# Moving the next step's scores, and two of the four down quarters, within TensorE's order of work

## The reference

```
h = layernorm(x) * (1 + ca) + sa
x = x + ga * attention(h)         # 16 heads of 8, causal, window of 32 keys
h = layernorm(x) * (1 + cb) + sb
x = x + gb * moe(h)               # 8 experts of 128 -> 256 -> 128
# moe: gate scores, the best 2 of 8 weighted by a softmax; per expert
#      y_e = layernorm(h + gelu(h @ w1_e + b1_e) @ w2_e + b2_e) * g_e + b_e
#      out = sum over e of weight_e * y_e
```

## Time and profile before

| what | value |
|---|---|
| median of 3 runs (lowest to highest) | 275.79 us (274.9 to 275.96) |
| the profiled execution's own time | 275.96 us |
| its span | 274.2 us |
| granted TensorE clock, mean | 0.966 of full speed |
| PE busy | 239.3 us, 87% |
| weight loads (PEld) busy | 206.0 us, 75% |
| DVE, ACT, POOL busy | 184.4, 159.8, 134.6 us |

### The profile page before, as it was taken

The page is one execution under the profiler, slowest core; times in us unless marked ns, Lnnn a source line. Parts: engine busy times, 40 slices in busy tenths (PEclk is TensorE's granted clock), DMA queues, the critical chain, the costliest instruction groups (busy, mean ns, idle before and its releaser), DMA issues.

```text
span 274.2 us, 7792 instructions
## 1 busy us (share of the span) xinstructions
PE 239.3 (87%) x3064; PEld 206.0 (75%) x3064; DVE 184.4 (67%) x570; ACT 159.8 (58%) x419; POOL 134.6 (49%) x254
## 2 busy tenths in 40 slices
PE   7985884999999989998999989999999899989970
PEld 4653554988888878887888878888888788767960
DVE  2778469548596758666876769485967585456075
ACT  2354402784579375956487548844893769455650
POOL 8065436024670477146732675256714770468075
PEclk9979896899999999999999999999999999999996
DMA  6930000000000000000000000000000000000000
GB/s 203 332 151 0 2 4 1 0 4 2 4 19 2 4 2 0 19 6 0 4 19 2 2 2 20 4 4 2 19 2 2 2 1 19 6 0 0 22 0 20
DMA packets 5652, 6.23 MB, mean 23 GB/s; under 512 B 336, under 2 KB 5104, under 8 KB 5360
## 3 DMA queue, kind: packets, MB, share of 16 engines
q1 hardware_dynamic: 5616, 5.74, 6.5%
HBM read 4.68 MB, written 1.05 MB: 21 GB/s over the span
## 4 chain that ended last, share of the span: by engine, by line
PE 48%; DVE 25%; ACT 15%; POOL 5%; issue 4%; DMA 1%; POOLq 0%; ACTq 0%; DVEq 0%
ACT hid L484 10%; PE score L976 6%; PE z L1004 6%; PE turns L867 6%; DVE q_st L590 6%; PE score L968 5%; PE turns L869 3%; PE turns L868 3%; ACT L445 3%; DVE ypart L660 3%; PE score L987 3%; DVE xn L570 2%; PE score L1048 2%; POOL rstd L340 2%; PE turns L913 2%
## 5 line engine op out<-in xcount | busy, mean ns | idle before, releaser
L484 ACT ACTIVATE hid<-turns,pack_ffn 128x256 f32<-128x256 f32 x128 | 50.6, 472 | 44.4 <-PE turns L869 44.4
L1004 PEld LDWEIGHTS z<-w,hid 128*128 128x128 f32 x480 | 59.3, 191 | 3.7 <-issue 1.0
L1004 PE MATMUL z<-w,hid 128*128 128x128 f32 x480 | 61.5, 276 | 0.0
L867 PE MATMUL turns<-h_hi,w_hi 128*128 128x256 f32 x128 | 40.8, 318 | 8.4 <-ACT hid L484 4.4
L309 POOL TENSOR_SCALAR zvar<-zss 128x4 f32<-128x4 f32 x32 | 6.2, 193 | 82.1 <-DVE zss L646 73.1
L323 POOL TENSOR_TENSOR ypart<-ypart 128x256 f32<-128x256 f32 (+1 forms) x60 | 35.9, 599 | 18.4 <-DVE ypart L660 15.4
L869 PE MATMUL turns<-h_hi,w_lo 128*128 128x256 f32 x128 | 37.0, 289 | 0.0
L868 PE MATMUL turns<-h_lo,w_hi 128*128 128x256 f32 x128 | 36.9, 289 | 0.0
L660 DVE SCALAR_TENSOR_TENSOR ypart<-z,zcoef,ln_gG 128x128 f32<-128x128 f32 x120 | 34.1, 341 | 1.8 <-POOL zcoef L314 1.7
L867 PEld LDWEIGHTS turns<-h_hi,w_hi 128*128 128x128 f32 x128 | 25.1, 196 | 13.0 <-ACT hid L484 8.7
L310 POOL TENSOR_TENSOR zrstd<-zvar,mhalf 128x4 f32<-128x4 f32 x32 | 33.1, 1033 | 2.7
(11 more groups left out here) (143 smaller groups left out, 457.3 us busy)
## 6 DMA issues: line engine op xcount, KB each, us to landing
w<-in_w SPq DMA_DIRECT2D x2, 1024.0 KB, 9.3
out_x<-yout SPq DMA_DIRECT2D x8, 128.0 KB, 1.8
x_tokens<-in_x SPq DMA_DIRECT2D x1, 896.0 KB, 6.8
ln_g<-in_ln_g SPq DMA_DIRECT2D x1, 512.0 KB
pack_mod<-in_pack_mod SPq DMA_DIRECT2D x1, 385.0 KB, 3.0
pack_proj<-in_pack_proj SPq DMA_DIRECT2D x1, 193.0 KB, 4.7
pack_att<-in_pack_att SPq DMA_DIRECT2D x1, 130.5 KB, 4.6
x_tokens<-in_x SPq DMA_DIRECT2D x1, 128.0 KB, 3.0
```

The costliest lines, as they stand in the source:

```text
L484: last = a.activation(hid[:, e, c, :], U[(e + 1) % 2][:, c * STEP:(c + 1) * STEP], ACT.Gelu, bias=b1[:, e, c:c + 1])
L867: mm(outp, a_hi, b_hi, start=True, stop=False)
L1004: last = mm(z_bank(f, q)[:, e * D:(e + 1) * D], hid[:, ee, c, tt * P:(tt + 1) * P], w2[:, ee * CH + c, :], start=False, stop=e == HALF - 1 ...
```

## The change

Three moves on TensorE; no instruction is added or removed, and the lists of the other engines stay as they are. The third quarter of the down products, `down(f, 2, ...)`, moves back: its first part behind `values(i, 3)` and `proj_v(n)`, its second part behind `out_proj(i)`. The next step's `scores(n)` move ahead of `turn_x2(i)`, in step 0 too. The last quarter, `down(f, 3, ...)`, moves from ahead of `turn_x2(i)` to behind it, but for step 7, where there are no next scores, and it stays ahead.

```diff
@@ -1124,14 +1124,12 @@
                 if nxt:
                     proj_k(n)
                     proj_q(n)
-                if ffn and att:
-                    down(f, 2, 0)
                 if att:
                     values(i, 3)
                 if nxt:
                     proj_v(n)
                 if ffn and att:
-                    down(f, 2, 1)
+                    down(f, 2, 0)
                 if i == STEPS - 1:
                     keep_warm_last(3)
                 if i == 0:
@@ -1141,17 +1139,21 @@
                 if i == 0:
                     keep_warm(8)
                 if ffn and att:
+                    down(f, 2, 1)
+                if nxt:
+                    scores(n)
+                elif ffn and att:
                     down(f, 3, 0)
                     down(f, 3, 1)
                 if att:
                     turn_x2(i)
-                if nxt:
-                    scores(n)
+                if nxt and ffn:
+                    down(f, 3, 0)
+                    down(f, 3, 1)
                 if i == STEPS - 1:
                     keep_warm_last(4)
                 if att:
                     gate(i)
-                if att:
                     up(i, 0)
                     up(i, 1)
                     up(i, 2)
```

## The result

| | before | changed |
|---|---|---|
| median (lowest to highest), 10 runs each | 275.88 us (274.48 to 276.58) | 277.87 us (276.58 to 278.32) |
| ratio, with its 95% interval | | 1.0074 [1.0048, 1.0099] |
| profiled execution, and its span | 275.96, 274.2 us | 277.93, 276.1 us |
| six full steps | 174.43 us | 175.74 us |

The change made the kernel slower by 2.0 us; 3.45 were forecast. The last line of the table is the distance between the exponentials' first table load in step 1 and that in step 7.

A forecast was written before the change was run, and what follows sets the result against it. Bound: PE's work between the second norm's turn and the gate, which delays the gelu. Full steps 2.7, step 0 0.65 and step 7 0.1 sum to 3.45 us on 275.96: 279.4 us, range 277.6 to 282.4.

The forecast's parts named there:

- The bound: Full steps: PE's work between the second norm's turn and the gate delays the gate, hence the gelu and the step.
- The block's own length: Last quarter's sixteen down loads on PE, moved behind the turn: 2.49 us, 0.43 more than the scores.
- The term that failed: Last quarter replacing the scores behind the turn: 0.45 us slower per full step, 2.7 us over six (2.4 to 4.0).
- The total: Whole kernel: 3.45 us slower, 279.4 us; bounds together 278.9 to 281.0, stated range 277.6 to 282.4.
- Two signs: Full steps in the profile after: gate 0.4 to 0.7 us later after the turn; steps of 29.5 to 29.7 us.
- Step 0: Scores behind the keep-warm products hold the turn, with no down quarter to fill the window: 0.65 us slower (0.5 to 0.75).
- Step 7: Last quarter stays ahead of the turn, half of the third is added there: 0.1 us slower (0 to 0.25).
- The covers: Output projection stays at 155.46, PE idle before it about 1.4 us; DVE keeps 0.7 us idle before the next weights.
- The longer block: Rival: last quarter's extra length behind the turn is hidden, only steps 0 and 7 cost: about 276.7 us; chance 0.11.
- DVE did not fall behind: Rival that DVE falls behind: shifts end over 0.7 us later than reckoned, delaying the next step's weights: 282.4 us; chance 0.05.
- The early output projection: Rival: values moved up free the output projection from 155.46 to 154.1, full steps gain 0.85 us: 271.6 us; chance 0.05.
- The falling clock: Rival: PE's longer pause before the output projection lowers its clock; six such steps make 292 us; chance 0.03.

The follow-up runs named there:

- The short sums: The change, but ACT sums the squares of only one of the last quarter's four experts in steps 0 to 6: ratio 1.0066.
- two experts ahead of the turn: Kernel before, but in full steps the scores and two of the last quarter's four experts ahead of the turn, the others behind: ratio 1.0064.
- the filled wait: The first split, with the third quarter wholly ahead of the output projection and the last quarter's first expert ahead of the scores: 269.75 us, ratio 0.9798.
- the first split: Kernel before, but in full steps the scores and the last quarter's first expert ahead of the turn, the other three behind: ratio 0.9996.

## Why the prediction was right, and too large

**The bound, right.** The gate's delay went into the gelu whole, and a step grew by as much as the block between turn and gate. The kernels with parts of the quarter moved show it one to one. The short sums show that ACT was not the bound of the change, and DVE kept idle time; DVE's split becomes the bound only with two experts ahead of the turn.

**The block's own length, right.** I worked out 2.49 us for the last quarter; the change has 163.24 - 160.76 = 2.48.

**The term that failed: 0.45 us a step, measured 0.22.** The step was "It takes the place that the scores left", from 159.67 on. In the row of the scores stands a pause of 0.17 us, which "From the turn on it has no pause" passes over, and I left it in the path as if whatever followed the turn had to wait for it. The pause went away with the scores. Behind the turn, down products begin after 160.76 - 160.59 = 0.17 us, the scores after 159.67 - 159.30 = 0.37. So the scores took 0.37 - 0.17 = 0.20 us more out of the path than their 2.06, and the difference is 2.48 - 2.06 - 0.20 = 0.22. Six times that is 1.3 us instead of 2.7. Neither end of my range for the term counted a pause onto the scores: the upper, 0.67, counted one onto the quarter, and the lower, 0.40, stood just under the plain difference of 0.43 without a reason of its own.

**The total, right in part by luck.** 277.87 us lies 1.0 us below 278.9, the lower bound of my sum. It is inside the range only because I had drawn that down to 277.6 for a block that is hidden in part, and nothing was hidden: the gate's delay was passed on whole. Two signs missed for the same reason: the gate came 0.22 us later after the turn instead of 0.4 to 0.7, and the steps are 29.3 us instead of 29.5 to 29.7.

**Step 0, right at the turn:** 0.65 us forecast, 4.43 - 3.77 = 0.66 there. That the first full step also began 0.65 us later in these two profiles is chance: with the old order of step 0 it begins between 52.70 and 54.20 in eight profiles, with the new one between 53.69 and 54.85 in three. Measured alone, step 0 costs 0.4 us with an interval from -0.2 to 1.0, so it is not shown that all of the 0.66 reaches the end.

**Step 7: 0.1 forecast, none measured;** the turn stands 248.16 - 244.32 = 3.84 us behind the output projection there, as before.

**The covers held.** The output projection stayed where DVE put it, with 1.24 us of idle PE before it (1.4 forecast); DVE kept 0.60 us of idleness before the weights (0.7 forecast).

**The rivals.** The longer block was not hidden, and DVE did not fall behind. The early output projection had no ground: DVE takes the attention without idle time. The falling clock was given 0.03 for the change, and the change's profile shows no fall in its full steps. But the reason I gave, that longer pauses had been survived, was too simple: with the scores alone moved, pauses of 0.88 and 0.43 us with the scores between them went with a fall in one step of twelve, though each is shorter than the 1.82 us after which the clock held.

## What to carry to other kernels

Where a block is moved off the path and another takes its place, subtract whole distances, from the end of what precedes to the start of what follows, pauses included; do not take a pause between two neighbours for a cost of the one that stays, until another order shows whose it is. List all waits of the moved instructions, also those that cost nothing today: the scores' wait for their bank was hidden behind the last quarter, and whoever moves the quarter has to fill it. When the path goes through one engine, cut the work that must stand behind its last wait, and put the rest into the waits before, as far as no other engine's list becomes the later one: here that was worth 2%, with the same instructions.

## What was not expected of the hardware

TensorE's clock fell to 1.2 GHz (granted 0.50) in the middle of a full step, in one step of twelve in two profiles of one kernel, for 3 us and more, and cost 1.6 us there; the other steps had pauses of 0.88 and 0.43 us or nearly the same, and kept 2.4 GHz. What decides between them stays open.

And the scores, whose loads have 32 rows, begin some 0.2 us later than full-size loads in the same place. They begin 0.37 us after the turn, where full-size loads begin after 0.17. In the change they begin 158.29 - 157.19 = 1.10 us after the start of eight down loads, where the gate in the kernel with two experts ahead follows eight such loads after 161.55 - 160.64 = 0.91. In the kernel with the filled wait they are late as well, 0.76 us after the start of four down loads where the turn of the first split follows four after 0.56, though DVE's copy, for which they wait, had ended 0.6 us earlier; so it is not that wait. That is shown in the orders tried here; its cause was not tested, and 32 rows need not be it: full-size loads behind v's projection, whose loads have 64 columns, also begin with an idle 0.17 us (153.85 in the change).
